# Reordering VectorE's routing work and TensorE's ranks' product in a linear-attention and mixture-of-experts layer

## The reference

```python
xn = layernorm(x)
# linear attention, 16 heads of 16
q, k, v = elu(xn @ Wq + bq) + 1, elu(xn @ Wk + bk) + 1, xn @ Wv + bv
kv  = einsum('bkhd,bkhm->bhdm', k, v)
out = einsum('bqhd,bhdm->bqhm', q, kv) / max(einsum('bqhd,bkhd->bqh', q, k), 1e-6)
att = out @ Wo + bo
# shared and routed feed-forward
shared = swiglu(xn @ w_in.T) @ w_out.T
g_probs = softmax(xn @ wg.T + gb)                # 2 groups, the better one is taken
p = softmax(e_logits where the group matches) * g_prob   # 4 experts in the group
topv, topi = top_k(p, 2)
h = swiglu(xn @ w1.T)
routed = sum over e of (h * w_se[:, e]) @ w2[e].T
return x + att + shared + routed
```

## Time and profile before

| what | value |
|---|---|
| median of 3 runs | 925.65 us (925.24 to 927.51) |
| the profiled execution | 925.4 us |
| its span, first to last instruction | 923.6 us |
| TensorE matmul busy | 904.0 us, 98% |
| VectorE busy | 698.7 us, 76% |
| GpSimd busy | 469.7 us, 51% |
| ScalarE busy | 367.6 us, 40% |

### The profile page before, as it was taken

The page is one execution under the profiler, slowest core; times in us unless marked ns, Lnnn a source line. Parts: engine busy times, 40 slices in busy tenths (PEclk is TensorE's granted clock), DMA queues, the critical chain, the costliest instruction groups (busy, mean ns, idle before and its releaser), DMA issues. The chain is left out here.

```text
span 923.6 us, 22859 instructions
## 1 busy us (share of the span) xinstructions
PE 904.0 (98%) x6982; PEld 815.9 (88%) x6983; DVE 698.7 (76%) x1816; ACT 367.6 (40%) x605; POOL 469.7 (51%) x550
## 2 busy tenths in 40 slices
PE   8899999999999999999999999999999999999995
PEld 7698988889898989888898989898889999999995
DVE  6988777787869687777878686877686777777773
ACT  5544534453535445344535354453431222222220
POOL 3756462635445364626354453544351666655564
PEclk9999999999999999999999999999999999999998
DMA  9432414131323324141323233241155777787760
GB/s 282 127 100 85 134 48 125 69 102 69 107 88 100 120 71 127 46 125 69 102 72 105 85 101 125 57 136 46 59 194 145 141 141 139 147 149 137 136 127 1
DMA packets 145912, 100.21 MB, mean 109 GB/s; under 512 B 55520, under 2 KB 136928, under 8 KB 145888
## 3 DMA queue, kind: packets, MB, share of 16 engines
q1 hardware_dynamic: 105312, 63.81, 23.9%
q0 software_dynamic: 17968, 25.32, 12.4%
q10 hardware_dynamic: 22608, 10.77, 4.2%
HBM read 53.29 MB, written 48.00 MB: 110 GB/s over the span
## 5 line engine op out<-in xcount | busy, mean ns | idle before, releaser
L347 PE MATMUL bank<-wexp_hi,xnT_hi 128*128 (+1 forms) x560 | 188.0, 336 | 1.8 <-DVE xnT_lo L1153 1.6
L349 PE MATMUL bank<-wexp_hi,xnT_lo 128*128 (+1 forms) x560 | 186.0, 332 | 0.0
L348 PE MATMUL bank<-wexp_lo,xnT_hi 128*128 (+1 forms) x560 | 185.8, 332 | 0.0
L1233 POOL TENSOR_TENSOR h_lo<-gated,h_hi 128x256 fp32r<-128x256 f32 x128 | 93.9, 760 | 83.6 <-ACT h_hi L712 83.3
L347 PEld LDWEIGHTS bank<-wexp_hi,xnT_hi 128*128 128x128 f32 x560 | 106.3, 190 | 14.9 <-issue 4.7
L349 PEld LDWEIGHTS bank<-wexp_hi,xnT_lo 128*128 128x128 f32 x560 | 106.4, 190 | 10.2
L348 PEld LDWEIGHTS bank<-wexp_lo,xnT_hi 128*128 128x128 f32 x560 | 106.5, 190 | 9.5
L1257 POOL TENSOR_TENSOR res<-res,bo_t 128x256 f32<-128x256 f32 x64 | 47.0, 764 | 113.7 <-DMA res<-x 113.7
L347 PE MATMUL bank<-xnT_hi,win_hi 128*128 128x512 f32 x256 | 101.9, 398 | 0.0
L348 PE MATMUL bank<-xnT_lo,win_hi 128*128 128x512 f32 x256 | 100.0, 391 | 0.0
L349 PE MATMUL bank<-xnT_hi,win_lo 128*128 128x512 f32 x256 | 100.0, 391 | 0.0
(11 more groups left out here) (194 smaller groups left out, 2423.2 us busy)
## 6 DMA issues: line engine op xcount, KB each, us to landing
res<-x SPq DMA_DIRECT2D x16, 512.0 KB, 3.6
out<-res SPq DMA_DIRECT2D x16, 512.0 KB, 3.0
xt<-x SPq DMA_DIRECT2D x15, 512.0 KB, 3.5
xn_d<-xt SPq DMA_DIRECT2D x15, 512.0 KB, 4.8
xt<-xn_d SPq DMA_DIRECT2D x60, 128.0 KB, 3.1
xt<-h_d SPq DMA_DIRECT2D x76, 64.0 KB
xt<-h_d ACTq DMA_DIRECT2D x76, 64.0 KB
kb<-h_d SPq DMA_DIRECT2D x76, 64.0 KB
```

The lines of the kernel that those rows point to most:

```text
L347: e.matmul(to, w_hi, m_hi_, start=first_, stop=False, skip_group_check=free)
L348: e.matmul(to, w_hi, m_lo_, start=False, stop=False, skip_group_check=free)
L349: return e.matmul(to, w_lo, m_hi_, start=False, stop=last_, skip_group_check=free)
L1233: ins = pool.tensor_tensor(h_lo[:, j, cols], gated[:, j % 2, cols], h_hi[:, j, cols].bitcast(f32), ALU.subtract)
```

## The change

In all batches but the last, VectorE takes phi(q), the key sums, the head masks and both first gates ahead of the choice of experts, then the choice, the norms, the transposes, routed gates 0 and 1, and only then the ranks and the table rows. In the last batch the order stays, but routed gate 0 moves behind the table rows. TensorE makes the ranks' product behind routed block 1 (in the last batch: where it was) and waits for routed gate 1 at the spread product, whose second bank that gate reads. GpSimd issues the fourth h scatter and, except in the last batch, the third `low` ahead of the third row scatter.

```diff
+            def ranks(b):
+                pe.wait_ge(oh_rdy, b + 1)
...
+                mm.then_inc(rt_done, 1)
...
                 routed(0, (3, 4))
 
-                pe.wait_ge(oh_rdy, b + 1)
...
-                mm.then_inc(rt_done, 1)
+                if last:
+                    ranks(b)
...
                 routed(1, (7, 2))
+                if not last:
+                    ranks(b)
...
                 pe.wait_ge(rn_rdy, b + 1)
+                pe.wait_ge(rg_rdy, TB * b + 2)
...
                 link(dve.tensor_tensor(cmq[:, :, :, :], cmp[:, :, :, :], wi, ALU.mult))
-                routed_gate(b, 0, 4)
                 dve.tensor_copy(pos_i[:, :], pos[:, :])
...
+                if last:
+                    best_two(b)
+                    head_sums()
+                    ranks_in(b)
...
+                    table_rows(b)
+                    routed_gate(b, 0, 4)
+                    value_blocks()
+                    routed_gate(b, 1, 2)
+                    norms()
+                else:
+                    head_sums()
+                    best_two(b)
+                    norms()
+                    value_blocks()
+                    routed_gate(b, 0, 4)
+                    routed_gate(b, 1, 2)
+                    ranks_in(b)
+                    table_rows(b)
                 routed_gate(b, 2, 1)
...
                 h_out(2)
+                h_out(3)
+                if not last:
+                    low(2, HC * b + 2, hhi_rdy, hlo_rdy)
                 row_out(2)
-                h_out(3)
                 row_out(3)
-                low(2, HC * b + 2, hhi_rdy, hlo_rdy)
+                if last:
+                    low(2, HC * b + 2, hhi_rdy, hlo_rdy)
                 low(3, HC * b + 3, hhi_rdy, hlo_rdy)
```

More of the change, by code:

```diff
@@ L492, in routed @@
                 mm.then_inc(rh_done, 1)
+            def ranks(b):
+                pe.wait_ge(oh_rdy, b + 1)
+                W = NSLOT
+                pe.matmul(bank[5][:, 256:256 + TB * W], triones[:, 0, :], oh[:, :, :].rearrange("p t c -> p (t c)"),
+                          start=True, stop=False, skip_group_check=True)
+                for n in range(TB, 0, -1):
+                    o = 256 + (TB + 1 - n) * W
+                    mm = pe.matmul(bank[5][:, o:o + n * W], triones[:, 1, :], oh[:, 0:n, :].rearrange("p t c -> p (t c)"),
+                                   start=False, stop=(n == 1), skip_group_check=True)
+                mm.then_inc(rt_done, 1)
             def batch(b, last):
@@ L1013, in batch @@
                 probabilities(b)
-                wait(dve, rt_done, b)
[L1015 to L1041, removed]
+                def head_sums():
+                    if first_row(b):
+                        dve.wait_ge(ffn_split, HC)
+                    for o in range(DC):
+                        dve.wait_ge(eq_rdy, DC * b + o + 1)
+                        wait(dve, nb_done, 3 * (b - 1) + 1)
+                        dve.tensor_tensor(phiq[:, o, :], expt[:, o, :], relut[:, o, :], ALU.add).then_inc(phiq_rdy, 1)
+                    acc = bank[2][:, 0:DC * (HP + 1)].rearrange("p (c n) -> p c n", c=DC)
+                    if first_row(b):
+                        dve.wait_ge(out_w_ld, 16 * 3)
+                    dve.wait_ge(acc_done, b + 1)
+                    dve.tensor_copy(ksum[:, :], acc[:, :, HP]).then_inc(kstep, 1)
+                    dve.wait_ge(kstep, KS * b + 1)
+                    for c in range(DC):
+                        ins = dve.tensor_scalar(khead[:, c, :], heads[:, c, :], ksum[:, c:c + 1], None, ALU.mult)
+                    ins.then_inc(kstep, 1)
+                    gate(b, 0, 7)
+                    for c in range(DC):
+                        ins = dve.scalar_tensor_tensor(kvm[:, c, :], bv[:, c, :], ksum[:, c:c + 1], acc[:, c, 0:HP],
+                                                       ALU.mult, ALU.add)
+                    ins.then_inc(kstep, 1)
+                    dve.wait_ge(kstep, KS * b + 3)
+                    dve.tensor_tensor(kvm[:, :, :], kvm[:, :, :], head.unsqueeze(1).broadcast_to([P, DC, HP]),
+                                      ALU.mult).then_inc(kvm_rdy, 1)
+                    gate(b, 1, 1)
@@ new lines, in norms @@
+                def norms():
+                    dve.wait_ge(nb_done, 3 * b + 1)
+                    dve.tensor_scalar(rn, bank[6][:, 0:P], EPS_N, None, ALU.max).then_inc(kstep, 1)
+                    dve.wait_ge(kstep, KS * b + 4)
+                    dve.reciprocal(rn, rn).then_inc(kstep, 1)
+                    dve.wait_ge(kstep, KS * b + 5)
+                    dve.tensor_copy(rhigh.bitcast(f32r), rn).then_inc(kstep, 1)
+                    dve.wait_ge(kstep, KS * b + 6)
+                    dve.scalar_tensor_tensor(rn, rhigh, low_row, rn, ALU.mult, ALU.add).then_inc(kstep, 1)
+                    dve.wait_ge(kstep, KS * b + 7)
+                    dve.tensor_tensor(rdiag, rn.unsqueeze(1).broadcast_to([P, TB, P]),
+                                      own_block.unsqueeze(2).broadcast_to([P, TB, P]), ALU.mult).then_inc(rn_rdy, 1)
@@ L1042, in batch, with value_blocks @@
+                def value_blocks():
+                    dve.wait_ge(kvm_rdy, b + 1)
+                    wait(dve, m_done, b)
+                    for i in range(4):
+                        rows = slice(HP * i, HP * i + HP)
+                        ins = dve.transpose(kvT[rows, :, HP * i:HP * i + HP], kvm[rows, :, :])
+                    ins.then_inc(kvT_rdy, 1)
+                wait(dve, rt_done, b)
                 if last:
+                    best_two(b)
+                    head_sums()
+                    ranks_in(b)
```

## The result

The changed kernel takes 1010.42 us (median of 4 runs, 1007.61 to 1010.93) against 925.76 us before in the same session: the ratio is 1.0905, with a 95% interval from 1.0888 to 1.0922. It is slower by 85 us. The forecast was 1001 us, in a range of 967 to 1025.

The account below looks back on a forecast made before the run. TensorE, busy 98% of the span, was taken as the bound. Stalls of 14 x 4.1 = 57.4, batch 0 6.6, batch 14 -1.4 and clock 13 gave +75.6 on 925.4 us: forecast 1001 us, range 967 to 1025.

Parts of the forecast that it names:

- The chain: VectorE's table rows release GpSimd's scatters, then the last `low`, which TensorE needs before its `m_hi` matmuls; 0.64 us to spare.
- 4.18 us of norms, kvT and routed gate 1 ahead of the table rows: On VectorE, 1.62 us of kvT and routed gate 1 plus 2.56 of norms move `row_rdy` from 293.45 to 297.63.
- the upper bound: Stall of 5.7 us a batch: 1.6 more if GpSimd's subtractions slow VectorE's choice of experts to 4.26 us.
- The rival in which the choice always takes the slow 4.26 us: VectorE's choice contends with GpSimd always and the clock falls always: 5.7 us a batch, up to 1039 us; chance 0.12.
- The size of the stall: TensorE waits for GpSimd's third and fourth `low`: 4.1 us a batch, in holes of 1.0 and 3.0 us.
- The clock: TensorE's clock falls behind the new 3.0 us hole once in two batches, 0.85 us a batch, 13 us in all.
- Batch 0: In the first batch `tok` ends at 46.3 instead of 39.6 us, giving 6.6 us of stall.
- Seams: On TensorE, one or two more changes between small and large matmuls, 0.1 us each, covered by the stall.
- Nothing for head sums and choice: On VectorE the two swap and end together at 290.48; phi(q), key sums and gates 2.67 us earlier gain nothing.
- the new wait of the spread product: TensorE's wait for routed gate 1 costs nothing: the gate ends near 295.3, the product stood at 298.28.
- The next batch's transposes: VectorE's transposes wait for the last h scatter, 2.9 us later, hidden since the next batch starts 4.1 us later.
- The signs: Expected evidence: `h_lo` waits some 60 us, two holes a batch, batches 46 to 47.5 us, `tok` at 15.5, clock below 1.00.

## Why the prediction was right, point by point

- *The chain.* Right: `row_rdy`, ten pieces on GpSimd, last `low`, `m_hi` matmuls. Shown by the order of GpSimd alone (1010.4 to 931.9 us).
- *4.18 us of norms, kvT and routed gate 1 ahead of the table rows.* Right in kind; `tok` came 5.0 us later (16.3 against 11.3). The prediction had head sums and choice swap places and end together, 8.33 us behind the value sums; they end at 9.25. The choice took 3.10 us (320.30 to 323.40) with GpSimd's lows beside it (319.25 and 321.12), not 2.67; phi(q) started later (1.7 us behind the value sums, not 1.5, where the choice used to be first) and took 1.50 until the key sums, not 1.20. Within the upper bound; in the sum it had been left out. The rival in which the choice always takes the slow 4.26 us did not come true: 3.10 is nearer to 2.67.
- *The size of the stall.* Forecast 4.1; measured 3.6 of holes and 0.2 of the seam, which the stall was to cover, though `row_rdy` was later than I had it. The term that was too large is GpSimd's own: 14.24 us for the ten pieces, measured 13.18 (331.37 to 344.55). A `low` follows a scatter without the 0.2 us that I had added, and two scatters are shorter than in the earlier trace rows; the last `low` is 0.5 longer, since `xnT_lo` on VectorE meets it.
- *The clock.* This term was mis-sized. I counted a fall in every second batch, 13 us in all; it fell in every one of batches 0 to 14: behind the second hole in batches 1 to 13, behind the first in batch 14 (2.6 us there, the second 1.8), and in batch 0 behind the hole at the ranks' product. Short of full are 30.2 us (0.970 of 1005.8) against 5.5 before (0.994 of 923.6): 25 us more, and filling the second hole brought back 24.
- *How near the sum came.* The clock was 12 us too small; against it the stalls were 4 too large (14 x 0.3) and batch 0 was 2 too large. The other 3 of the 9 us between forecast and result are within what the runs differ by: the profiled execution, from which these terms are read, is the fastest of the four (1007.6 us), the others have clocks of 0.967 and 0.968. That the forecast came within 1% is thus in part luck, since its errors had opposite signs.
- *Batch 0.* From its value sums to the next it took 51.53 us against 46.06, 5.5 more; forecast 6.6 and 0.85 of clock. Its waits are in part other ones than I had named: 2.35 us at the ranks' product for the choice, 2.25 at the `m_hi` matmuls, and the old one at the head product.
- *Seams.* 0.16 us a batch (42.48 against 42.32), within 0.1 to 0.2.
- *Nothing for head sums and choice, nothing for the new wait of the spread product.* For the first: TensorE has no wait for phi(q) or the key sums in a steady batch, but the later end of the choice was not nothing; it is most of the 0.8 us above. The second shows in the waits of the changed kernel, in which the spread product is not named.
- *The next batch's transposes.* Hidden, as said: no wait of TensorE for `xnT_lo` between batch 0 and the end of the loop. Not free for others, though, since `xnT_lo` (342.73, 2.38 us instead of 1.30) lengthens the last `low`.
- *The signs.* Two holes a batch came, and the clock fell. A batch takes 47.7 to 47.9 us, just above the 46 to 47.5 named, for a fall in each; `tok` ended at 16.3 instead of 15.5; the waits for `h_lo` are 48.8 us, not 60.
- What stays open: why the clock falls behind a hole in some batches and not in others of the same kernel. With GpSimd's old order in the changed kernel it fell behind the hole in 10 of 15 batches: among batches 1 to 13 in six of nine with a hole of 3.2 us, in both with 2.6, in neither with 2.0.

## What to carry to other kernels

Before a step is moved ahead of another on an engine with time to spare, look for who waits for the step that now comes later, through other engines as well, and how much that chain has to spare: here 0.64 us against 4.18. On an in-order engine an instruction has both a place and an input: moving it ahead of its input costs what stands behind it (29 us here, from one `low` and one scatter that changed places with others), moving it behind costs its waiter. When a dense TensorE gets a hole of 2 to 3 us in each repetition, put the fall of its clock into the price: here it added 1.7 us to 3.6, in every batch.

## What the runs showed of the hardware

- How often the clock fell behind a hole of TensorE, batches 1 to 13, one hole a batch: 1.9 us, in none of 13 (GpSimd's order moved alone) and in one of 13 (norms behind the table rows); 3.2 us, in six of nine. Behind a hole of 2.9 us that follows 1.4 us after one of 0.7 it fell in 13 of 13; with 1.5 us of small matmuls in the larger one, in none of 13. In batch 0 it fell behind a hole of 1.9 us too. So the length of the hole alone does not decide.
- A fall cost 1.7 us: the granted clock was 0.85, 0.50 and 0.79 in three stretches of 2 us.
- GpSimd and VectorE slowed each other, in large operations too: GpSimd's `low` took 1.90 and 2.37 us instead of 1.43, and VectorE's pair of `xnT_lo` 2.38 instead of 1.30, when they met.
